# Attention: the second score product in the steepest head group alone, exponentials in query blocks with biases of their own; two other additions

## What is computed

```python
q = _l2norm(q) * q_scale
k = _l2norm(k) * k_scale
sim = jnp.einsum('bhid,bhjd->bhij', q, k) * ATTN_SCALE
dist = -jnp.abs(cols[None, :] - (rows[:, None] + NUM_NULL_KV)).astype(sim.dtype)
sim = sim + dist[None, None] * slopes[None, :, None, None]
sim = jnp.where(causal_mask[None, None], neg, sim)
attn = jax.nn.softmax(sim, axis=-1)
```

## Time and profile before

| | |
|---|---|
| median of 3 runs | 1755.71 us (1751.26 to 1756.75) |
| profiled execution | 1750.87 us, span 1749.1 |
| TensorE busy | 1565.2 us (89%), mean granted clock 0.946 |
| VectorE, ScalarE, GpSimd busy | 1036.5, 774.6, 596.5 us |
| preparation of turn 0 | to 65.9 us |
| 16 attention turns | 65.9 to 1228 us |
| first MoE layer | to 1376 us |
| last stage | 1376 to 1749 us |

### The profile page before, as it was taken

How to read it: one execution, slowest core, us unless ns; L and a number is a source line. 1 busy time by engine, 2 the same in 40 slices (tenths; PEclk the granted TensorE clock), 3 DMA queues, 4 the chain that set the end, 5 groups by cost and what they waited for, 6 DMA issues and landing times. The chain is left out here.

```text
span 1749.1 us, 28227 instructions
## 1 busy us (share of the span) xinstructions
PE 1565.2 (89%) x8941; PEld 740.7 (42%) x8941; DVE 1036.5 (59%) x2399; ACT 774.6 (44%) x1364; POOL 596.5 (34%) x597
## 2 busy tenths in 40 slices
PE   5799999999999999999999999999399549888898
PEld 2344444444444444444444444444267334333332
DVE  4455646666565655657656566665523277777775
ACT  3345454454544445544454444544144234444432
POOL 4253452534436354353543515442300331111000
PEclk8799999999999999999999999999599759999999
DMA  3502030320202202021120200000411100000000
GB/s 109 170 7 76 23 99 1 111 70 1 70 4 73 61 28 70 1 70 37 41 76 1 70 8 6 10 3 6 158 48 55 38 13 7 13 13 13 7 7 13
DMA packets 106718, 73.77 MB, mean 42 GB/s; under 512 B 5250, under 2 KB 100762, under 8 KB 106319
## 3 DMA queue, kind: packets, MB, share of 16 engines
q1 hardware_dynamic: 104526, 67.76, 12.7%
q0 software_dynamic: 2048, 4.20, 0.8%
HBM read 24.23 MB, written 47.71 MB: 41 GB/s over the span
## 5 line engine op out<-in xcount | busy, mean ns | idle before, releaser
L826 ACT ACTIVATE P<-S,keyb 128x386 f32<-128x386 f32 (+7 forms) x512 | 296.6, 630 | 375.8 <-PE S L609 375.6
L605 PE MATMUL S<-QT,KT 64*128 64x512 f32 (+5 forms) x1792 | 378.5, 478 | 8.3 <-DVE KT L964 6.3
L1200 POOL TENSOR_TENSOR rn<-nm,half 128x12 f32<-128x12 f32 x128 | 299.5, 2344 | 94.4 <-DVE nm L901 94.4
L1223 POOL TENSOR_SCALAR_AFFINE_SELECT P<-P 128x256 f32<-128x256 f32 (+1 forms) x256 | 156.3, 611 | 478.9 <-ACT P L826 478.7
L1004 DVE TENSOR_TENSOR Psum<-Psum,P 128x1796 f32<-128x1796 f32 (+7 forms) x256 | 281.9, 1101 | 37.5 <-PE O L630 18.3
L630 PE MATMUL O<-P,V 128*64 128x512 f32 (+5 forms) x1536 | 255.4, 436 | 4.0 <-POOL P L1223 3.3
L605 PEld LDWEIGHTS S<-QT,KT 64*128 64x128 f32 (+1 forms) x1792 | 158.4, 179 | 193.2 <-issue 183.6
L609 PE MATMUL S<-GQ,GK 64*128 64x512 bf16 (+5 forms) x896 | 150.9, 303 | 0.0
L466 PE MATMUL W<-xT,wts 128*128 128x512 f32 x256 | 141.3, 646 | 9.8 <-DVE QT L960 7.2
L1071 DVE TENSOR_TENSOR part<-W,rden 128x512 f32<-128x512 f32 x128 | 82.4, 686 | 83.4 <-PE W L678 83.4
L630 PEld LDWEIGHTS O<-P,V 128*64 128x64 f32 (+1 forms) x1536 | 80.0, 135 | 108.6 <-issue 94.2
(11 more groups left out here) (244 smaller groups left out, 2118.6 us busy)
## 6 DMA issues: line engine op xcount, KB each, us to landing
xg<-zero SPq DMA_DIRECT2D x16, 1216.0 KB, 10.6
yg<-zero SPq DMA_DIRECT2D x16, 1216.0 KB, 9.6
wts<-in_w_qkv SPq DMA_DIRECT2D x16, 384.0 KB, 3.8
gu<-in_gu SPq DMA_DIRECT2D x1, 2816.0 KB, 10.4
xb<-xg SPq DMA_DIRECT2D x40, 64.0 KB, 1.8
yg<-yb SPq DMA_DIRECT2D x40, 64.0 KB, 1.6
X<-in_x SPq DMA_DIRECT2D x4, 512.0 KB, 4.5
wo<-in_w_out SPq DMA_DIRECT2D x16, 128.0 KB, 2.3
```

Of the source, the lines that this page charges most:

```text
L605: nc.tensor.matmul(S[hh][0:m, at + c:at + c + w], KT[d, r, p, jt * P:jt * P + m], QT[d, r, p, Q0[jt] + c:Q0[jt] + c + w], start=True, stop ...
L826: nc.scalar.activation(probs(p, jt)[0:m, hh, 0:n], S[hh][0:m, at:at + n], ACT.Exp, bias=keyb[0:m, r, (2 * p + hh) * NKT + jt:(2 * p + hh) ...
L1200: nc.gpsimd.tensor_tensor(rn[:, c, u], nm[:, c, u], powers, ALU.pow).then_inc(rn_ok, 1)
L1223: nc.gpsimd.affine_select(own, own, [[0, 2], [1, w]], ALU.is_ge, 0.0, base=NNULL if jt == 0 else 0, channel_multiplier=-1).then_inc(cut, 1)
```

## The change

- Groups 1 to 3 (`FLAT`) drop the second score product, the edge transposes and their copies, and in `parts` the five `ee`/`E` operations and their rounds. A turn whose group is in `FLAT` is called flat below.
- There the whole bias sits in the exponential's bias, as if the query stood in the middle of its block. Where the slope is too steep for 1024 queries, a head's queries are cut in blocks with an exponential and a bias column each: 4, 2, 2, 1 blocks for the heads of group 1, one elsewhere. `tabs` grows from 36 to 81 key columns per group, and a bound on the score, worked out at the start (`lim`), is subtracted.
- Turn 0's inverse norms come from a square root on ScalarE and seven small VectorE operations, not from GpSimd, and the laps and `parts` of turn 0 stand earlier.
- In the last stage TensorE does `share` after `down`, turns the normed rows and routes one slot earlier; VectorE chooses experts in slots 4 and 5 and weighs in slots 6 and 7; chunk 1 is gathered later.
- Some tiles (`w1qt`, `w1v`, `w1m`, `blk`) now lie in the first exponential buffer.

```diff
+def width(h):
+
+    w = SEQ
+    while slopes()[h] * w / 2 >= LIFT:
+        w //= 2
+    return w
+
+
+FLAT = tuple(g for g in range(NG) if width(HG * g) >= 2 * P)
+BLOCKS = [[SEQ // width(HG * g + h) if g in FLAT else 1 for h in range(HG)] for g in range(NG)]
+KEYS = NKT * max(sum(n) for n in BLOCKS)
+TAB = KEYS + TT * HG
...
     for g in range(NG):
-        h = slice(g * HG, g * HG + HG)
-        tab[:, g] = np.concatenate([key[:, h].reshape(P, -1), qry[:, :, h].reshape(P, -1)], axis=1)
+        for h in range(HG):
+            for b in range(BLOCKS[g][h]):
+                middle = b * width(HG * g + h) + width(HG * g + h) // 2
+                at = NKT * (sum(BLOCKS[g][:h]) + b)
+                pos = P * kt[None, :] + p[:, :, 0] - NNULL
+                tab[:, g, at:at + NKT] = sl[HG * g + h] * (pos - middle) + LIFT if g in FLAT else key[:, HG * g + h]
+        tab[:, g, KEYS:] = qry[:, :, g * HG:g * HG + HG].reshape(P, -1)
...
+            def flat_turn(n):
+
+                return n % NG in FLAT
+
+            def edged(n, c):
+
+                return sum(0 if flat_turn(m) else 14 for m in range(n)) + (0 if flat_turn(n) else 7 * c + 7)
...
-                return [k for k in AT if k[0] != "X" or n - 1 in HALF_AT]
+                return [k for k in AT if (k[0] != "X" or n - 1 in HALF_AT) and not (k in EDGE and flat_turn(n))]
...
-            AT_LAPS = {6: (2, 3), 9: (4, 5), 13: (6, 7)}
-            DVE_LAPS = {4: (2, 3), 9: (4, 5), 13: (6, 7)}
-            ACT_LAPS = {7: (2, 3), 10: (4, 5), 14: (6, 7)}
+            AT_LAPS = {6: (2, 3), 8: (4, 5), 9: (6, 7)}
+            DVE_LAPS = {4: (2, 3), 6: (4, 5), 8: (6, 7)}
+            ACT_LAPS = {7: (2, 3), 8: (4, 5), 10: (6, 7)}
...
-                            nc.tensor.matmul(S[hh][0:m, at + c:at + c + w], KT[d, r, p, jt * P:jt * P + m],
-                                             QT[d, r, p, Q0[jt] + c:Q0[jt] + c + w], start=True, stop=False)
-                        for hh in range(2):
+                            last = nc.tensor.matmul(S[hh][0:m, at + c:at + c + w], KT[d, r, p, jt * P:jt * P + m],
+                                                    QT[d, r, p, Q0[jt] + c:Q0[jt] + c + w], start=True, stop=flat_turn(t))
+                            if flat_turn(t) and c + w == n:
+                                last.then_inc(qk, 1)
+                        for hh in range(0 if flat_turn(t) else 2):
...
+                        pe.wait_ge(lim_ok, 3)
+                        nc.tensor.matmul(S[1][:, 512:512 + P], rows_n[:, 0:P], rows_n[:, P:2 * P], start=True, stop=True)
...
-                        nc.scalar.activation(probs(p, jt)[0:m, hh, 0:n], S[hh][0:m, at:at + n], ACT.Exp,
-                                             bias=keyb[0:m, r, (2 * p + hh) * NKT + jt:(2 * p + hh) * NKT + jt + 1]).then_inc(exp_ok, 1)
+                        g, h = t % NG, 2 * p + hh
+                        blocks = BLOCKS[g][h]
+                        for b in range(blocks):
+                            lo = max(Q0[jt], b * SEQ // blocks - (NNULL if b else 0)) - Q0[jt]
+                            hi = ((b + 1) * SEQ // blocks - NNULL if b + 1 < blocks else SEQ) - Q0[jt]
+                            col = NKT * (sum(BLOCKS[g][:h]) + b) + jt
+                            if lo < hi:
+                                last = nc.scalar.activation(probs(p, jt)[0:m, hh, lo:hi], S[hh][0:m, at + lo:at + hi], ACT.Exp,
+                                                            bias=keyb[0:m, r, col:col + 1])
+                        last.then_inc(exp_ok, 1)
...
+                    act.wait_ge(prep_ev[BANK[TURNED[c]]], emptied(0, TURNED[c]))
+                    if c:
+                        act.wait_ge(step_ok, 7)
+                    hold(act)
+                    nc.scalar.activation(flat[:, 0], nm[:, c].rearrange("p u n -> p (u n)"), ACT.Sqrt).then_inc(flat_ok, 1)
...
+                def first_roots(c):
+
+                    y, a_, b_ = flat[:, 1], flat[:, 2], flat[:, 3]
...
+                    k = 7 * c
+                    dve.wait_ge(flat_ok, c + 1)
+                    nc.vector.tensor_scalar(b_, flat[:, 0], 1e-15, None, ALU.max).then_inc(step_ok, 1)
+                    dve.wait_ge(step_ok, k + 1)
...
+                    nc.vector.tensor_tensor(out, y, a_, ALU.mult).then_inc(step_ok, 1)
...
+                    nc.vector.tensor_tensor(rn[:, c, :, 2 * HG:], rn[:, c, :, 2 * HG:], nm[:, c, :, 2 * HG:],
+                                            ALU.mult).then_inc(step_ok, 1)
+                    dve.wait_ge(step_ok, k + 7)
+                    dve.sem_inc(rn_ok, 4)

...
+                nc.vector.tensor_scalar(rows_n[:, P:2 * P], idf[:], lim[:, 1:2], None, ALU.mult).then_inc(lim_ok, 1)
...
+                nc.vector.tensor_reduce(lim[:, 2:3], S[1][:, 512:512 + P], AX.X, ALU.max).then_inc(lim_ok, 1)
                 nc.vector.tensor_copy(w1q[:, 1, :], S[1][:, 0:D]).then_inc(m_ok, 1)
+                dve.wait_ge(lim_ok, 4)
+                keys = tabs[:, FLAT[0]:, 0:KEYS]
+                nc.vector.tensor_scalar(keys, keys, lim[:, 2:3], None, ALU.subtract).then_inc(lim_ok, 1)
...
-                    nc.gpsimd.tensor_tensor(rn[:, c, u], nm[:, c, u], powers, ALU.pow).then_inc(rn_ok, 1)
+                    w = (2 if flat_turn(n) else 3) * HG
+                    nc.gpsimd.tensor_tensor(rn[:, c, u, 0:w], nm[:, c, u, 0:w], powers[:, 0:w], ALU.pow).then_inc(rn_ok, 1)
...
-                        if s == at:
+                        if s == at and n:
...
-                    if j == 0:
-                        if live(u - 1):
-                            form(u - 1)
-                        if live(u - 2):
-                            combine(u - 2)
-                    elif live(u - 2):
-                        share(u - 2, j)
+                    if j == 0 and live(u - 1):
+                        form(u - 1)
+                    if j == 0 and live(u - 2):
+                        combine(u - 2)
                     if 0 <= k - LAG < KS:
                         down(k - LAG)
                     if j == 0 and live(u):
                         rows_turned(u)
-                    if j == 0 and live(u - 2):
-                        share(u - 2, 0)
+                    if live(u - 2):
+                        share(u - 2, j)
                     if j == 1 and live(u):
                         project(u)
                     if j == 2 and live(u - 3):
                         last_turned(u - 3)
+                    if j == 2 and live(u - 1):
+                        normed_turned(u - 1)
                     if j == 3 and live(u - 1):
-                        normed_turned(u - 1)
-                    if j == 4 and live(u - 1):
                         route(u - 1)
                     if j == 8 and live(u):
                         sums_turned(u)
...
                         norm2.scalar_apply(act, y2, X[:, u - 1], u - 1)
...
-                    if j == 4 and live(u + 1):
-                        arrive(u + 1)
-                    if j == 6 and live(u):
-                        weigh(u, 1)
-                    if j == 8 and live(u - 1):
-                        weights(u - 1)
                     if live(u - 2):
                         gated(u - 2, j)
                     if j == 0 and live(u - 1):
...
                         shared(u - 2, j)
                     if j == 2 and live(u - 3):
                         ended(u - 3)
+                    if j == 3 and live(u - 1):
+                        logits(u - 1)
+                    if j == 3 and live(u + 1):
+                        arrive(u + 1)
                     if j == 4 and live(u - 1):
-                        logits(u - 1)
+                        pick_one(u - 1)
+                        pick_other(u - 1)
+                    if j == 5 and live(u - 1):
+                        weights(u - 1)
                     if j == 5 and live(u):
                         shares(u)
-                        weigh(u, 0)
-                    if j == 6 and live(u - 1):
-                        pick_one(u - 1)
-                    if j == 7 and live(u - 1):
-                        pick_other(u - 1)
+                    if j in (6, 7) and live(u):
+                        weigh(u, j - 6)

...
                         norm2.pool_shift(pool, u - 1)
                     if j == 2 and live(u - 3):
                         norm1.pool_shift(pool, n4(u - 3))
-                    if j == 4 and live(u + 1):
+                    if j == 3 and live(u + 1):
                         norm.pool_shift(pool, n2(u + 1))
+                        if u < 0:
+                            get_chunk(1)
                         if live(u + 3):
                             get_chunk(u + 3)

                 for k in range(4):
                     pool.wait_ge(st_y[k], 16 * NBLK // 4)
                 get_chunk(0)
-                get_chunk(1)
                 periods(slot)
```

(3 more changed lines are left out.)

105 lines of the change are left out of this document (71 added, 34 removed).

## The result

The changed kernel takes 1723.87 us (median of 4 runs, 1720.87 to 1725.06) against 1753.49 us (4 runs, 1750.06 to 1756.75): ratio 0.9829, 95% interval 0.9803 to 0.9855, or 29.6 us less. I had forecast 1694 us in a range of 1664 to 1714. The sign was right, and half of the gain is missing; the time lies above the range. The span of the profiled execution is 1719.2 us, 29.9 less than before.

A forecast was written before the change was run, and what follows sets the result against it. TensorE was taken to bound attention turns, VectorE their end stretch and much of the last stage's period. Terms 56.7 - 2 - 5 + 4 + 5 = 58.7 us off 1750.9 gave 1692; median forecast 1694, range 1664 to 1714.

The forecast's parts named there:

- Clock: Turn starts: longer TensorE waits make about three more starts dip, 5 us lost, bounds 0 and 19.
- Rival (b): Lost clock: all 15 turn starts dip and the last stage dips twice per period, +20 us, 1714 us; chance 0.18.
- Rival (c): Slower than before: low clock lasts through VectorE's whole stretch, 7 us late in each of 15 turns, 1799 us; chance 0.03.
- The rule against the change: Skill's rule: matmul bursts short against waits swing the clock, so every turn start and last-stage period would lose clock.
- grow by the rest: Turn's end: VectorE's stretch shortens 0.7 us, TensorE's list there 1.1, so TensorE's two waits grow by the difference.
- The product's price: Second score product: 0.22 us per head pair and 512 queries, 3.42 us of each flat turn's TensorE-bound part.
- The signs: Expected in the changed profile: VectorE still gapless at turn ends, flat turns of 67 to 70 us, steep 71 to 74.
- Exponentials in blocks: Turns 1, 5, 9, 13: added ScalarE instructions cost 0.5 us per turn, 2 us in all, bounds 0 and 16.
- Preparation: Turn 0: square root replacing GpSimd's powers brings first scores earlier, net 4 us gained, bounds 0 and 9.
- Turn 15 and the gather of chunk 1: Turn 15 gets 4.0 us shorter, and the later gather frees GpSimd 1 us earlier.
- Last stage: Second MoE layer: periods of 39.5 us instead of 41.0, 8.7 us gained before the first period's loss, net 5.
- The first period: Last stage, first period with expert choice: choice and weights now precede attention weighing, so it ends 4.7 us later.

The follow-up runs named there:

- runs 2 and 8: Score product repeated as filler ahead of TensorE's wait for RT or the choice, on the changed kernel (1701.26 us) and the kernel before (1748.58 us), respectively.
- run 7: Changed kernel with the score product repeated ahead of the wait, and one exponential per head and key tile in turns 1, 5, 9, 13: 1700.86 us.
- run 12: Changed kernel with the preparation of turn 0 put back as before: 1726.32 us, one execution.
- run 10: Kernel of run 9 with the last stage's gate and up products of slots 7 and 8 computed twice: 1698.30 us.
- run 5: Changed kernel with VectorE's additions at the turn's end split in three places, so neither RT nor KT is late: 1702.51 us.
- run 11: Kernel before with VectorE's additions at the turn's end split in three places: 1754.52 us.
- run 9: Changed kernel with split additions, light filler, and weighing ahead of choice in the last stage's first period with expert choice: 1696.32 us.

## Why the prediction was right in its sign and wrong in its size

**Clock: the step that failed.** I wrote that three more turn starts would dip, 1.7 us each, "5 us lost. Bounds 0 and 19 us". Ten turn ends dipped, the lost clock rose by 31.9 us, and single dips cost up to 5.1 us instead of 1.7. Filling the wait won 19.9 us of the attention (1085.7 to 1065.8) with 28.5 us less clock lost, so some 0.7 us of time per microsecond of clock. By that the clock cost about 22 us, beyond my upper bound. This is an estimate from one pair of traces (the filler shortened no wait for free: it put work in its place). The bound of the term was the fault: I took the only length of a spell in the trace (9 us at 0.81) as the length of any spell. Rival (b) named the mechanism and priced it from the same row. Rival (c) had considered low clock "through VectorE's whole stretch" and set it aside because nothing in the trace showed it; in turns 9, 10, 13 and 14 it came to most of that, ten microseconds at half clock.

**The rule against the change.** The trace shows dips at 10 of 15 turn ends, none of them behind a wait above 1.94 us. The Trainium skill (TensorE: Matmul & The Clock Gate, HAM oscillation — how this bites in real kernels) describes a kernel whose bursts of matmuls, about 2 us, are shorter than its waits for DMAs, 3 to 5 us, and whose clock falls behind every wait. Here bursts of tens of microseconds stood against waits of under 2 us, which is not that case. The clock fell all the same: the rule pointed the right way, I priced it too low, and its reason does not fit this case.

**Waits "grow by the rest", 0.4 us.** Too small. TensorE's waits over the whole turn grew from 2.9 to 4.6 us in turn 6, and from 2.2 to 3.4 in turn 3. The five corrections of a flat turn took 1.45 us (263.37 to 264.82 in turn 2), not 1.2: 0.29 us per dependent step, not the 0.25 that I took without a row. Waits for `part` and `rows_n` and pauses in issue came up too, 1.0 us in turn 3 where there had been 0.2, in steps that I had counted as TensorE-bound. So the turns that ran at full clock gained 2.3 (turn 3), 1.1 (4), 3.6 (6), 2.8 (7) and 2.2 us (11), the last two with the 1.7 us dip of before taken off: 12.0 where my terms give 3.42 + 1.25 + 4.67 + 3.42 + 3.42 = 16.2. The product's price (0.22 us per 512 queries) was right: TensorE's busy time fell by 3.6 us in turn 3 and by 5.4 in turn 6, where product and transposes come to 4.0 and 5.1. A quarter of what it frees turned into waits. The filled pair agrees: with all their lost clock taken off, the attentions of runs 2 and 8 are 41.9 us apart (40 with 0.7 of it), of 52.7 predicted. The 11 us missing here and the 17 missing in the clock term, less the 2 us that exponentials did not cost, make 26 of the table's 26.7 us; with the 40 it would be 28, so the split between waits and clock is good to about 2 us.

**The signs.** VectorE was not gapless at the turn ends that lost clock, against what I wrote, and flat turns took 69.7 to 75.6 us instead of 67 to 70. **The upper end of the range** rests on a wrong sum: rival (b) names 14 us at the turn starts and, in the last stage, five times 2.4 us and no gain. The first two alone are 26 us and with the 8.7 us of gain withdrawn 35, not 20, so (b) is about 1729 and not 1714. With that end the measured 1724 us would have lain in the range, but by luck, since the last stage did not lose as (b) says.

**Exponentials in blocks**: 2 us charged, none found (run 7). **Preparation**: 4 against 3.5, by terms whose sizes run 12 gives only roughly (-5.7 and +2.2). **Turn 15 and the gather of chunk 1**: 5.0 against 5.05, a match of the sum; its parts were not tried alone. **Last stage**: periods of 38.2 to 39.9 us, mean 39.1 (39.5 predicted), with waits of 0.2 to 1.9 us for `hid` and `o` that sum to 4.2 us in some periods and to 2.6 in others, instead of one of 4.50 (rows 12). I had forecast 4 to 6 us in four pieces of 1 to 2. That VectorE is behind in slots 2 to 7 and TensorE in slots 8, 0 and 1 fits run 10. But I said that "only the 2.4 us of clock can be won": run 10's period at full clock is 38.2 us, 2.7 less than before, and low clock at a period's start costs 1.7. How much of this is VectorE's order and how much clock no run separates. The first period was mis-sized, 7.0 against 4.7 us.

## What to carry to other kernels

Work taken from TensorE in front of a wait is partly turned into waiting (here a quarter of it), and where TensorE is the bound, the longer wait can cost more than its own length in clock; look for what stands in VectorE's list ahead of the copy that TensorE waits for and need not stand there. Repeating a matmul ahead of the wait is a cheap test of whether the clock matters in a place: 22.6 us in the attention, 4.9 us in the middle periods of the last stage. Read such a test stretch by stretch: in the last stage the filler cost 6.6 us where no wait stood behind it, and the total hid the gain. Price such a dip by what it costs if it lasts to the end of the stretch, not by the one in the trace.

## What was not expected of the hardware

Waits of 1.7 to 1.9 us were enough for the half clock, and the same wait in the same code did it in some turns and not in others: turn 6 waited 1.93 us at full clock, turns 9 and 10 lost 5.1 us each behind it. Each dip at a turn's end came to 1.7, 3.4 or 5.1 us of lost clock. What decides between them stays open. Nor do waits have to be long: in run 5, turn ends with several waits, the longest 0.8 or 1.0 us, were followed by the half clock in eight turns, and in run 11 two turn ends lost 5.1 us of clock each with no wait over 0.7 us.

Where the half clock falls decides its price: 1.7 us of lost clock cost 1.7 us at the start of a last-stage period (39.9 us against 38.2, run 9) and nothing near its end (38.2 us at a granted clock of 0.96, changed kernel).
